# A window-attention layer and a state-space layer on one core: three convolution parts moved to later slots, one depthwise tap moved from TensorE to VectorE

## The reference

```
x  = x + dwconv3x3(x)                          # layer 0
q, kv = split(layernorm(x) @ qkv_w)            # windows of 8 x 8, 7 x 7 windows
idx = top_k(mean(q) . mean(k), 4)              # 4 windows per window
o  = softmax(q . k[idx]) @ v[idx]              # 4 heads
o  = (o + dwconv5x5(v)) @ wo_w                 # the 25 taps ("lepe")
x  = x + o ;  x = x + mlp(layernorm(x))
y  = conv3x3(x)                                # layer 1
s  = y.reshape(pixels, 8 tokens, 16)           # a sequence of 8 tokens per pixel
xi, z = split(s @ in_proj) ; xc = silu(causal_conv1d(xi, 4 taps))
dt, B, C = ... ; h = exp(dt*A)*h + dt*B*xc ; out = (h . C + D*xc) * silu(z) @ out_proj
x  = x + silu(groupnorm(out))
```

## Time and profile before

| | us |
|---|---|
| median of 3 runs | 10573.59 |
| lowest, highest | 10556.45, 10581.08 |
| profiled execution | 10566.67 |
| its span | 10564.6 |

### The profile page before, as it was taken

The page is one execution under the profiler, slowest core; times in us unless marked ns, Lnnn a source line. Parts: engine busy times, 40 slices in busy tenths (PEclk is TensorE's granted clock), DMA queues, the critical chain, the costliest instruction groups (busy, mean ns, idle before and its releaser), DMA issues. The chain is left out here.

```text
span 10564.6 us, 200712 instructions
## 1 busy us (share of the span) xinstructions
PE 8593.4 (81%) x61658; PEld 3655.3 (35%) x61658; DVE 8682.6 (82%) x10568; ACT 6501.9 (62%) x12597; POOL 6485.6 (61%) x4046
## 2 busy tenths in 40 slices
PE   6999999999899998877887877788887777787870
PEld 3555555555555554222222222222222222222220
DVE  6777777777777775999989999998989999998985
ACT  5666666666666665666656666665666666666653
POOL 3222222222222221888888898988888888888980
PEclk9999999999999998888888898988888889888885
DMA  2222322222322322111111111111111111111119
GB/s 68 69 69 70 77 71 69 69 69 71 80 74 73 75 74 52 33 41 33 37 37 33 36 39 33 41 33 33 40 35 33 41 33 36 39 33 35 40 40 277
DMA packets 855792, 591.01 MB, mean 56 GB/s; under 512 B 621424, under 2 KB 725872, under 8 KB 848464
## 3 DMA queue, kind: packets, MB, share of 16 engines
q1 hardware_dynamic: 751440, 423.61, 17.3%
q0 software_dynamic: 49152, 100.76, 2.6%
q10 hardware_dynamic: 54016, 51.91, 1.6%
HBM read 109.27 MB, written 103.81 MB: 20 GB/s over the span
## 5 line engine op out<-in xcount | busy, mean ns | idle before, releaser
L1217 POOL TENSOR_TENSOR b_hh<-b_hh,b_cn 128x1024 f32<-128x1024 f32 x1600 | 3833.7, 2414 | 496.0 <-DVE b_hh L1516 495.6
L1516 DVE TENSOR_TENSOR_SCAN b_hh<-b_dA,b_ub 128x512 f32<-128x512 f32 x2800 | 3369.6, 1206 | 0.0
L278 POOL DMA_DIRECT2D kvsel<-kv x1536 | 1103.1, 721 | 2885.3 <-issue 2455.3
L1357 ACT ACTIVATE b_dA<-b_db,b_negA 128x448 f32<-128x448 f32 x2800 | 1719.3, 633 | 1289.3 <-PE b_db L1609 1280.8
L1501 DVE TENSOR_TENSOR b_ub<-b_ub,b_bn 128x512 f32<-128x512 f32 x2800 | 1904.5, 680 | 543.2 <-PE b_ub L1609 528.0
L1609 PE MATMUL b_ub<-b_rows,b_pick 96*64 96x512 bf16 x6400 | 1407.6, 441 | 946.3 <-DVE b_hh L1516 901.3
L1609 PE MATMUL b_db<-b_rows,b_pick 96*64 96x512 bf16 x6400 | 1283.8, 424 | 203.5 <-ACT b_dA L1357 199.8
L1609 PEld LDWEIGHTS b_ub<-b_rows,b_pick 96*64 96x64 bf16 x6400 | 361.3, 110 | 3130.9 <-DVE b_hh L1516 2668.6
L554 DVE SCALAR_TENSOR_TENSOR oacc<-vpad,vec,oacc 128x1064 f32<-128x1064 f32 (+1 forms) x934 | 1199.7, 1302 | 11.4
L1645 PE MATMUL b_acc<-b_hh,b_gather 64*32 64x512 f32 x12800 | 1008.5, 692 | 3.0 <-POOL b_hh L1217 3.0
L395 ACT ACTIVATE prob<-score,nmax 128x256 f32<-128x256 f32 (+1 forms) x1600 | 735.9, 478 | 167.3 <-issue 96.1
(11 more groups left out here) (190 smaller groups left out, 13559.5 us busy)
## 6 DMA issues: line engine op xcount, KB each, us to landing
b_rows<-b_term SPq DMA_DIRECT2D x2400, 64.0 KB, 2.0
kvsel<-kv SPq DMA_DIRECT2D x1600, 64.0 KB, 2.1
kvsel<-kv POOLq DMA_DIRECT2D x1536, 64.0 KB
xpad<-in_x SPq DMA_DIRECT2D x18, 1568.0 KB, 10.7
ys<-ysb ACTq DMA_DIRECT2D x16, 1600.0 KB, 9.4
b_yc<-ys SPq DMA_DIRECT2D x100, 256.0 KB, 2.7
xr<-b_xo SPq DMA_DIRECT2D x100, 256.0 KB, 2.7
x<-x3pad SPq DMA_DIRECT2D x16, 1568.0 KB, 18.2
```

What stands on the lines that cost most here:

```text
L278: eng.dma_start(kvsel[:, slot, j, :, WPIX * t:WPIX * (t + 1)].unsqueeze(1), kv[:, bass.ds(at[t], 1), :, :]).then_inc((s_kv, s_kg)[j][slot] ...
L1217: nc.gpsimd.tensor_tensor(out=now, in0=now, in1=cn[:, par, :].unsqueeze(1).broadcast_to([C, 2, HT]), op=ALU.mult).then_inc(s_pm, 1)
L1357: nc.scalar.activation(later(dA[:, k % DEEP, :]), later(db[k % 2][:, :]), ACT.Exp, scale=negA[:, 8 * q + e:8 * q + e + 1]).then_inc(s_a, 1)
L1516: nc.vector.tensor_tensor_scan(hh[:, k // 2 % PDEEP, HT * (k % 2):HT * (k % 2 + 1)], rate, new, 0.0, ALU.mult, ALU.add).then_inc(s_sc, 1)
```

## The change

```
-        PTAP = 5
+        PTAP = 4
         VTAP = LEPE_TAPS - PTAP
...
-                    if s in (25, 26, 28) and before_end(n, 2):
-                        conv_even(n + 2, (25, 26, 28).index(s))
+                    if s in (27, 29, 30) and before_end(n, 2):
+                        conv_even(n + 2, (27, 29, 30).index(s))
```

## The result

The changed kernel takes 10383.95 us (median of three runs, 10377.38 to 10391.21) against 10573.59: a ratio of 0.983, with a 95% interval of 0.981 to 0.985. The forecast was 10570 with a range that began at 10500. The gain is real, and it lies outside the range.

The account below looks back on a forecast made before the run. VectorE was taken to bound the chunks, with TensorE late at places, and no engine to be full in the images. Chunks -10 and images +10 us left 10566.7; the median's 7 us made 10573, rounded to 10570, range 10500 to 10640.

Parts of the forecast that it names:

- Price of a chunk of each kind: Chunk stage, by wait ahead of product 29: short chunks gain 0.1 us, long ones 0.4, middle ones lose 0.9 to 1.1.
- The road over channel 30: Chunks: channel 30's repeat passes through ScalarE's exponential before scan 30; of a long chunk's 2.64 us only some 0.4 remain gained.
- Rival A: Chunks: the waits go and do not come back; half of 132 us gained, 10517 us; chance 0.28.
- The sum: Chunk stage: 54 x 0.1 + 35 x 0.4 - 10 x 0.95, about 10 us gained.
- the prediction's own sign for A: Chunks: a chunk mean under 59.8 us would show that waits go and do not come back.
- Middle chunks lose 0.95: 10 chunks where the clock returns during the first part: it returns one stretch later, 0.9 to 1.1 us lost each.
- Bounds of the stage: Chunk stage: at best the whole 132 us gained, at worst 98 us lost if short chunks stay at 1.2 GHz.
- VectorE's half of the tap: Images: three more VectorE products per image delay ScalarE; +0.44 us and, ahead of merges, +1.3 us per image.
- the price of a double ahead of a merge: Images: two VectorE products ahead of a merge cost ScalarE 1.04 us, the transposes that follow 0.81 and 0.82 more.
- TensorE's half: Images: two-tap steps become one-tap, 0.3 us gained in three of six (-0.9), last group's fifth tap -0.2, per image.
- Rival B: Images: VectorE's added taps are paid in full, 62 us lost, 10 gained on chunks, 10625 us; chance 0.16.
- Rival C: Chunks: slots 24 to 27 become light, the clock falls in short chunks too; 98 us lost, 10681, half 10632; chance 0.16.

Follow-up runs that it names:

- e1: Kernel before with only the tap changed (four on TensorE, 21 on VectorE), convolution in its old slots; ratio 0.9906.
- e3: Kernel before with one of 25 taps left out: TensorE four, VectorE its old 20, slots as before; ratio 0.9877.
- e8: Kernel before, word for word, profiled once more; one time, 10540.7 us.
- e10: Kernel before with TensorE's five taps spread 2, 1, 1, 1 over a group's four steps instead of 1, 1, 2, 1; ratio 1.0023.
- e2: Kernel before with only the convolution's parts moved to slots 27, 29, 30, five taps on TensorE; ratio 0.9919.
- e5: Changed kernel with the pairs carrying two VectorE products chosen anew, so that no merge has two ahead of it; ratio 0.9836.
- e11: Changed kernel with three taps on TensorE (steps 0, 1, 2) and 22 on VectorE; ratio 0.9891.
- e16: Changed kernel, unchanged, profiled once more; one time, 10415.2 us.
- e13: Kernel before with the convolution's parts in slots 25, 29, 30, so only the second and third move; ratio 0.9899.
- e4: Kernel before with the convolution's three parts in slots 29, 30 and 31, five taps; ratio 0.9933.
- e9: Kernel before with the convolution's first and third part cut to one column, the second made in full, old slots; ratio 0.9980.
- e6: Kernel before with three added TensorE products per chunk that nobody reads, in slots 20, 21, 22; ratio 1.0026.
- e7: Changed kernel with three added TensorE products per chunk that nobody reads, in slots 20, 21, 22; ratio 0.9836.

## Why the prediction was wrong

- **Price of a chunk of each kind: right.** For the short chunk scan 30 was put at 7667.6 to 7667.7, 5.9 to 6.0 us behind scan 26; 77 of the changed kernel's 99 chunks have 5.9 to 6.2. For the long one 8.7 us was worked out; the 20 long ones have 8.4 to 8.6. The road over channel 30 is there: scan 30 waits for ScalarE in 92 chunks, 23.1 us in all, and product 31 in the long ones, 2.2 us each. Rival A in its full form (waits go and don't come back) is wrong by that.
- **The failed step of the chunk stage: the counts.** The sum was 54, 35 and 10 chunks times a price each. The counts were taken over from the old order, with the sentence "TensorE does the same work before that point but for the second and third part, and by then the old order had its clock back". Over five executions of each order the late and middle chunks together are 38 to 47 of 99 in the old (before, e1, e3, e8, e10) and 17 to 30 in the new (changed, e2, e5, e11, e16). With the counts of before and the new prices (short 6.12 to 5.93, long 9.10 to 8.53, middle 7.75 to 8.53 if it is taken as long), the gain between scan 26 and 30 would be 53 x 0.19 + 36 x 0.57 - 10 x 0.78 = 23 us; measured are 89. So some 66 of them are the counts; by the means of five executions it is 12 of 68, so 56. Rival A had named this, "A shift of the chunks against the clock could also turn long chunks into short ones", and put no price on it; the mean chunk of 58.9 us is below 59.8, the prediction's own sign for A. What goes with the early share is the first part's place: with it in slot 25, 51 to 63 of 99 chunks are early (before, e1, e3, e8, e10, e13), with it moved or gone 69 to 90 (changed, e2, e4, e5, e9, e11, e16). The clearest pair is e13 and e2, which differ in nothing else. How it does that was not found.
- **"Middle chunks lose 0.95": not borne out.** Had "I expect the clock to come back one stretch later" come true for them, the late chunks would have become some 46. They are 20 and 28, and one or two middle chunks are left where 10 and 19 were.
- **Bounds of the stage.** Measured over five executions each, the order is worth 89 us, within the bounds -132 to +98; only the single pair of profiles (-141) is outside. The range at the end was cut from the inside: A was given "half of the 132", and the images could then not add to it. Even both stages at their bounds, 132 and 32 us gained, give 10409, above the 10384 measured.
- **VectorE's half of the tap: the sum right, by luck in part.** +0.44 and +1.3 us per image were predicted, 1.7; e1 against e3 gives 1.6. It is a difference of larger moves: the step of pair 5 is 1.3 us longer, as predicted, that of pair 4 0.9 shorter. And 0.81 and 0.82 us of the earlier trace rows were read as the price of a double ahead of a merge. They are TensorE's low clock in step 14: the second and the third image run this step at full clock, with the same 1.04 us ahead of it, and there the first of the two waits is not seen and the second is 0.16. ScalarE in the second image:

```profile
442.60 0.91 ACT L405 ACTIVATE prob<-prob,rinv 128x256 f32<-128x256 f32 x2 [1.04 <-DVE rinv L532]
...
448.15 0.47 ACT L395 ACTIVATE prob<-score,nmax 128x256 f32<-128x256 f32 x1 [0.16 <-DVE nmax L525]
```

- **TensorE's half: the mis-sized term.** "-0.9 and -0.2" per image; e3 gives -4.2 to -5.5. I had read the relief of a two-tap step from the waits recorded behind one such step (0.17 and 0.20) and given it to three of six. In e3's fifth image (the one of the earlier trace rows) the intervals between maxima at steps 4, 8, 12, 16 and 20 are shorter by 0.40, 0.32, 0.92, 0.57 and 0.56 us than before: it counts at all of them, and in the mean of the 16 images it is the same 2.8 us. Another 1.4 to 1.9 us per image are the steps at 1.2 GHz, of which before has 28, e8 22 and e3 8; the prediction had no term for the clock in the images. Neither bound (2 us gained at most) held the sum. The wait of the maximum for the scores, 210.8 us of the row L525, was not looked at; it is the row that carries this price, and it lost 72 us with the tap.
- **Rival B** is refuted at 21 taps (48 x 1.3 = 62 us of work cost 26) and comes true at 22 (e11). **Rival C**, and with it the rule of the Trainium skill ("TensorE: Matmul & The Clock Gate", section "HAM oscillation — how this bites in real kernels"), gave the wrong sign here: the moved parts did not leave slots 25 to 28 throttled, the granted clock of 0 to 4 us behind scan 26 rose from 0.77 to 0.89. What the rule says of bursts with waits between them does show elsewhere: in e9, with work taken out, the clock falls a second time in the chunk (0.69), and in the images it falls in 28 of the 48 steps behind an idle time of 2.0 us. That the clock falls at the chunk's end in e6, where work was added, the rule does not tell.

The two stages over all executions: the images end at 4172 in the mean with five taps (before, e2, e4, e6, e8, e9 and e13) and at 4125 with four (changed, e1, e7 and e16), -48 us. The chunks take 5956 with five taps in the old order (before, e8, e10) and 5844 with four in the new (changed, e5, e16), -112 us. Together that is -160. The medians' 190 us hold a before at the slow end of its own runs (in the later sets its medians were 10527 to 10560).

## What to carry to other kernels

A price per case times a count of cases is only as good as the count: where the cases are clock levels, the order of the work sets the counts, and neither leaving some of it out (e9) nor filling a gap (e6) gains until one looks at where the clock falls next. A wait read in one pass of a loop can be the clock's: compare it with a pass at full clock before it is made a price (the 0.81 and 0.82 us above). Before moving a tap off an engine, read the wait that the next engine pays for it over the whole stage (here the maximum's wait for the scores), not the one behind a single step. And a share that helps by one unit (five taps to four) can turn with the next (four to three).

## What was not expected of the hardware

- Taking two of three products (512 and 256 of 1152 columns) out of every chunk gained 0.2%, and the three moved two or three slots later 0.8%.
- Three idle-time products per chunk raised the granted clock of the chunk stage from 0.88 to 0.92 and made the kernel 0.3% slower (e6); the same three on the changed order took it from 0.90 to 0.94, with 32 us off the chunk stage of the profiles and no clear change of the median (e7).
- The same step of the attention, behind the same idle 2.0 us of TensorE, ran at 1.2 GHz in 28 of 48 cases and at full clock in the others: 5.9 us against 4.3.
- The same chunk code took between 5898 and 5969 us in five profiled executions, in step with the number of chunks whose clock came back late (18, 20, 28, 28 and 36).
